# Two graph layers on one core: the degree products spread over ten edge steps, the sums added nine steps late, the attention finished one chunk at a time

## The chip, the cores and the metric

The kernel runs on one core of one Trainium2 chip. Its time is the device time of one execution in microseconds. The kernel before takes 1850.17 us, the median of three runs from 1849.44 to 1851.53 us.

## The reference

Two graph layers run on 50,000 nodes of 256 float32 features with 12,500 edges. The first layer is an attention over the edges, the second a weighted graph convolution with self-loops and a small perceptron. Cut to what is computed:

```python
x_norm = layernorm(h) * g + b             # h = relu(layernorm(x))
q, k, v = x_norm @ Wq.T + bq, x_norm @ Wk.T + bk, x_norm @ Wv.T + bv
dk, dv = silu(edge_attr @ Wdk.T + bdk), silu(edge_attr @ Wdv.T + bdv)
attn = silu(sum(q[dst] * k[src] * dk, axis=1)) * cosine_cutoff(edge_weight)
msg = v[src] * dv * attn[:, None]
x1 = x + h + segment_sum(msg, dst) @ Wo.T + bo
# second layer, h = relu(layernorm(x1)), edges (src -> dst) plus a self-loop per node
deg = segment_sum(edge_weight, src) + 1
norm = rsqrt(deg[src]) * edge_weight * rsqrt(deg[dst])
h7 = segment_sum((h @ W)[dst] * norm, src) + h @ W / deg + b
out = x1 + relu(h7 @ W1 + b1) @ W2 + b2
```

## The kernel before

Edges are cut into 98 chunks of 128, the partitions of the chip's local memory; two chunks are a pair, so there are 49 pairs. The program has four stretches: an opening, the edge stage of the first layer (`messages`, one pair per step), the edge stage of the second layer (`messages2`, four chunks per step) and the node stage (`nodes`, 512 nodes per step). The change touches the first two.

Each engine has its own instruction list, written out by hand, and they meet only at semaphores. A Python function `messages(s)` describes one step for one engine. `Step.back(n)` is the pair that entered the pipeline n steps earlier, so step s works on several pairs at once. `run_steps` writes the first and last steps out and runs the middle ones in a hardware loop.

**The opening.** The degree of a node is a sum over edges. For every chunk VectorE makes two one-hot matrices (`hot`, L625 and L626) and TensorE multiplies them (L1178) and accumulates all 98 products in one bank. TensorE makes 48 of them, folds weights together (L1191 to L1204) and makes 50 more before its first edge step. VectorE makes 80 before its first step and 18 within steps 1 to 3. At the same time SyncE issues 98 stores of 512 KB (L394) that fill the table `sums0` with the output bias, and then one store per later use; no sum may be added before that fill has landed. Below it is called the fill.

**One edge step, for pair k.** GpSimd issues four gathers of 128 rows (L492): normalised source and destination rows come from them. VectorE takes statistics (L708, L710), ScalarE subtracts the mean (L1074, L1075), VectorE takes statistics again (L774), GpSimd raises the variance to the power of -0.5 (L523, the list calls it the power), ScalarE scales (L1054) and TensorE transposes (L1227), ScalarE copies the transposed rows to `zT` (L1024). For each chunk i of the pair TensorE then makes the edge product D (L1239), the product of keys and values (L1246, "KV" below) and the query product (L1253). ScalarE applies Silu to D (L1042, tile `ds`). VectorE multiplies keys (L718, `kd`), sums query times key (L723, `at`), ScalarE applies Silu (L1091, `sa`), and VectorE multiplies with the cutoff (L810, `aa`) and makes the message (L815, `msg`). TensorE sums messages of equal destination with equality matrices (L1269 to L1271, "S"), multiplies with Wo (L1285, "U"), ScalarE copies out (L1034, `ub`), and GpSimd adds two blocks of 128 rows to `sums0` (L488, the scatters).

TensorE's list in one step is: D, KV and query of chunk 0; transposes of chunk 1; S of the pair before; D, KV and query of chunk 1; U of two pairs before; transposes of chunk 0 of the next pair. GpSimd's list in step p is: gathers of pair p, scatters of pair p-7, power of pair p-2. The attention of both chunks is finished together at the end of VectorE's step: one Silu, one `aa`, both messages. Two buffers carry the rows of a scatter.

The loads of a pair's edge features and destinations (L370, L375) are on SyncE's list. Those of pairs 0 and 1 come first, those of pairs 2 and 3 stand between the stores of the fill, and those of pair 4 and later behind it, each with two more stores of 512 KB for the second table (L383).

```python
            for i in range(NG):
                if i in (LOADS_AT, LOADS_AT + 12):
                    load_edges(Step(2 + (i - LOADS_AT) // 12))
                sp.dma_start(group(sums0, Step(i)), rows_b).then_inc(s_fill, 16)
```

The inverse square roots of the degrees (`inverse_roots`, L681 to L687) stand behind VectorE's step 5.

## Time and profile before

| what | value |
|---|---|
| median of three runs | 1850.17 us (1849.44 to 1851.53) |
| the profiled execution | 1868.97 us |
| its span, first to last instruction | 1867.3 us |
| TensorE busy | 1629.1 us, 87% |
| VectorE busy | 1412.2 us, 76% |
| GpSimd busy | 1227.1 us, 66% |
| ScalarE busy | 1119.3 us, 59% |
| mean granted TensorE clock | 0.939 of full |

A busy share over the whole span hides that the four stretches have different limits: the profile's slices show the transfers at nine tenths or more for the first three slices of 47 us, and at seven, six and five tenths in those that follow. So the opening and the edge stage are read on their own, from windows, from the engines' timelines and from waits. In a row of a timeline stand start, length, engine, line, operation, output and input, the number of merged instructions, and in brackets the engine's idle time before it with what ended it. A float32 matmul appears as two records of TensorE. The end of a matmul is modelled.

### The profile page before, as it was taken

To read this page: it belongs to the slowest core of one execution; us is meant where nothing else is said; L and a number is where in the kernel's file an instruction comes from. 1 tells how busy PE (TensorE), PEld (TensorE's weight loads), DVE (VectorE), ACT (ScalarE), POOL (GpSimd) and SP (SyncE) were. 2 spreads that over 40 slices of the span, in tenths; PEclk is the share of its full clock that TensorE was granted. 3 is DMA by queue.
4 is the path that set the end of the run, shared out by engine and by line. 5 is a ranking of instruction groups with operands and counts; after the bars stand their busy time and mean duration, and the time that the engine had idled before them with its cause. 6 is when DMAs were issued, how large, how long until landed. Compare 5 with 4: busy or idle time off the path is not lost.

```text
span 1867.3 us, 29386 instructions
## 1 busy us (share of the span) xinstructions
PE 1629.1 (87%) x6406; PEld 1099.9 (59%) x6406; DVE 1412.2 (76%) x5503; ACT 1119.3 (60%) x2092; POOL 1227.1 (66%) x864
## 2 busy tenths in 40 slices
PE   8788999999999967676675169999999999999998
PEld 4355666666666635454454046666666666666666
DVE  7986777777777639777776497888888888888873
ACT  0155555556666522222222378889889889989984
POOL 3246777777777646888887765666666666666650
PEclk9999999999999987878777679999999999999999
DMA  9997666666666655555556678999999999999981
GB/s 370 419 415 244 175 175 174 174 174 175 177 177 185 195 136 115 118 111 108 113 115 126 136 200 248 255 266 271 269 268 268 267 270 267 267 268 269 274 230 75
DMA packets 148023, 398.67 MB, mean 214 GB/s; under 512 B 20144, under 2 KB 56756, under 8 KB 147974
## 3 DMA queue, kind: packets, MB, share of 16 engines
q1 hardware_dynamic: 89830, 280.18, 43.8%
q0 software_dynamic: 56416, 115.46, 32.8%
q10 hardware_dynamic: 1728, 2.50, 0.4%
q8 instruction: 15, 0.25, 0.1%
q14 instruction: 34, 0.28, 0.0%
HBM read 217.84 MB, written 180.23 MB: 213 GB/s over the span
## 4 chain that ended last, share of the span: by engine, by line
PE 27%; POOL 25%; issue 13%; DMA 11%; DVE 10%; ACT 7%; another core or an unknown queue 4%; SPq 3%; ACTq 0%; DVEq 0%; POOLq 0%
POOL sums_dram L488 9%; DMA out_dram<-cg 8%; PE bank L1361 6%; PE bank L1350 6%; POOL kept L578 6%; PE bank L1246 4%; POOL cg L492 4%; POOL b_rs L484 4%; ACT z L1054 4%; DVE cg L958 3%; PE bank L1178 2%; PE bank L1253 2%; PE bank L1340 2%; SPq L394 1%
## 5 line engine op out<-in xcount | busy, mean ns | idle before, releaser
L1350 PE MATMUL bank<-kept,w 128*128 128x512 f32 x784 | 355.4, 596 | 0.0
L1361 PE MATMUL bank<-w_sb,kept 128*128 128x256 f32 x1568 | 354.3, 379 | 0.0
L578 POOL TENSOR_TENSOR kept<-kept 128x1024 f32<-128x1024 f32 x98 | 232.4, 2371 | 183.4 <-DVE cg L958 183.4
L1361 PEld LDWEIGHTS bank<-w_sb,kept 128*128 128x128 f32 x1568 | 297.9, 190 | 81.9 <-issue 46.4
L488 POOL DMA_INDIRECT sums_dram<-ub,sidx x148 | 244.1, 1649 | 91.3 <-issue 42.3
L1314 PE MATMUL bank<-cg,en 128*128 128x256 f32 x386 | 132.8, 489 | 124.7 <-issue 80.6
L484 POOL TENSOR_TENSOR b_rs<-b_ve,minus_half 128x8 f32<-128x8 f32 x102 | 210.5, 2064 | 28.7 <-DVE b_ve L975 28.7
L1350 PEld LDWEIGHTS bank<-kept,w 128*128 128x128 f32 x784 | 142.6, 192 | 142.3 <-issue 142.3
L1145 ACT ACTIVATE kept<-kept,b_nb,b_rs 128x256 f32<-128x256 f32 x392 | 202.2, 588 | 21.9 <-DVE b_nb L948 21.9
L1246 PE MATMUL bank<-qkv_w,zT 128*128 128x512 f32 x392 | 192.0, 612 | 21.4 <-DVE msg L815 18.0
L1135 ACT ACTIVATE kept<-kept,b_nb,b_rs 128x256 f32<-128x256 f32 x392 | 202.2, 589 | 12.5 <-DVE b_nb L948 12.5
L1314 PEld LDWEIGHTS bank<-cg,en 128*128 128x128 f32 x386 | 94.2, 251 | 157.6 <-issue 139.6
L986 DVE SCALAR_TENSOR_TENSOR kept<-cg,dinv,kept 128x256 f32<-128x256 f32 x392 | 164.0, 480 | 5.1 <-issue 2.2
L1126 ACT ACTIVATE kept<-bank 128x1024 f32<-128x1024 f32 x98 | 100.4, 1024 | 90.6 <-PE bank L1340 90.6
L492 POOL DMA_INDIRECT cg<-in_x_dram,node_i x98 | 105.4, 1075 | 74.3 <-ACT cg L1075 48.7
L1340 PE MATMUL bank<-identity,kept 128*128 128x128 f32 x784 | 105.3, 278 | 54.7 <-DVE kept L986 54.4
L958 DVE TENSOR_TENSOR cg<-kept,bank 128x1024 f32<-128x1024 f32 x98 | 119.6, 1220 | 41.1 <-PE bank L1361 34.7
L1246 PEld LDWEIGHTS bank<-qkv_w,zT 128*128 128x128 f32 x392 | 71.3, 192 | 132.2 <-issue 72.3
L1024 ACT ACTIVATE zT<-bank 128x512 f32<-128x512 f32 x98 | 58.3, 595 | 144.2 <-PE bank L1227 79.6
L718 DVE TENSOR_TENSOR kd<-bank,ds 128x256 f32<-128x256 f32 x98 | 41.6, 424 | 130.4 <-PE bank L1246 73.2
L963 DVE BATCH_NORM_STATS2 b_st<-kept 128x6 f32<-128x256 f32 x392 | 137.0, 412 | 0.0
L967 DVE BATCH_NORM_STATS2 b_st<-kept 128x6 f32<-128x256 f32 x392 | 136.1, 410 | 0.0
(172 smaller groups left out, 3260.3 us busy)
## 6 DMA issues: line engine op xcount, KB each, us to landing
sums_dram<-cg SPq DMA_DIRECT2D x196, 512.0 KB
kept<-in_x_dram SPq DMA_DIRECT2D x97, 512.0 KB, 5.7
kept<-sums_dram POOLq DMA_DIRECT2D x97, 512.0 KB, 9.8
cg<-sums_dram SPq DMA_DIRECT2D x97, 512.0 KB, 8.7
out_dram<-cg SPq DMA_DIRECT2D x97, 512.0 KB, 9.8
row_d<-in_dst_dram SPq DMA_DIRECT2D x49, 128.0 KB
row_k<-keys_dram SPq DMA_DIRECT2D x24, 256.0 KB
row_s<-in_src_dram SPq DMA_DIRECT2D x24, 256.0 KB
```

The lines of the kernel that those rows point to most:

```text
L484: pool.tensor_tensor(to, var, minus_half[:, 0:width].rearrange("p (a b) -> p a b", b=1), ALU.pow).then_inc(done, 1)
L488: pool.indirect_dma_start(sums, bass.IndirectOffsetOnAxis(idx, 0), rows, None, bounds_check=bound, compute_op=ALU.add).then_inc(done, 16)
L492: pool.indirect_dma_start(to, None, table, bass.IndirectOffsetOnAxis(idx, 0), bounds_check=bound, oob_is_err=True).then_inc(done, 16)
L578: pool.tensor_tensor(X1[k.slot(8)], X[k.slot(4)], H[k.slot(2)], ALU.add).then_inc(g_xh, 1)
L958: dve.tensor_tensor(OUT[k.slot(2)], X1[k.slot(8)], bank[:, to:to + 2, :].rearrange("p a b -> p (a b)"), ALU.add).then_inc(g_fin, 1)
L986: ins = dve.scalar_tensor_tensor(AG[k.slot(2)][:, at0], S1[k.slot(4)][:, at0], dinv[:, bass.ds(k.value(0, G) + j, 1)], H1[k.slot(2)][:, at ...
L1135: ins = act.activation(H1[k.slot(2)][:, j * D:(j + 1) * D], X1[k.slot(8)][:, j * D:(j + 1) * D], ACT.Relu, bias=b_nb[k.back(-4).slot(2)][: ...
L1145: ins = act.activation(H[k.slot(2)][:, j * D:(j + 1) * D], X[k.slot(4)][:, j * D:(j + 1) * D], ACT.Relu, bias=b_nb[k.slot(2)][:, j, :], sc ...
L1246: ins = pe.matmul(bank[:, 2 + i, :], zT[i][:, c, :], qkv_w[:, c, D:3 * D], start=(c == 0), stop=(c == KC - 1))
L1314: ins = pe.matmul(bank[:, 6 * q + to // 2, (to % 2) * D:(to % 2 + 1) * D], EN[q][i][:, to * P:(to + 1) * P], H1e[q][:, i, :], start=(i == to),
L1350: ins = pe.matmul(bank[:, 2 + m, :], w01[:, c, m * P:(m + 1) * P], hT[k.slot(2)][:, c * GN:(c + 1) * GN], start=(c == 0), stop=(c == KC - 1))
L1361: ins = pe.matmul(to, rT[k.slot(2)][:, c * GN + j * P:c * GN + (j + 1) * P], w2_sb[:, c, :], start=False, stop=(c == KC - 1), skip_group_c ...
```

## The change

Five things change.

- `hots(step)` gives VectorE and TensorE the products of a step: 10, 8, 8, 8, 11, 11, 11, 11, 10, 10. TensorE makes 18 before its first step and folds the weights. The other 80 stand within steps 2 to 9, on TensorE behind the query product of chunk 1. The one-hot matrices have six buffers instead of four, and their sum is in bank 7. `degrees()` stands behind step 10 and `inverse_roots()` behind step 12.
- GpSimd scatters pair p-9 in step p. In steps before 11 the power comes ahead of the scatters. The rows of the first eight pairs lie in eight buffers, those of later pairs in four, made from tiles that are used later.
- The attention is finished per chunk: the query products of both chunks share bank 4, ScalarE applies Silu per chunk, VectorE makes the message of chunk 0 in the middle of its step and that of chunk 1 in the next step, behind the first statistics.
- TensorE transposes chunk 0 of the next pair ahead of U.
- ScalarE issues the loads of pairs 2 to 9, three steps behind their number. SyncE's fill has no loads in it, and the first 12 stores of the second table follow it without a load between them.

```diff
-HOT_FIRST, HOT_LOOPS = 48, 80
-HOT_STEP = 6
-LOADS_AT = 72
+HOT_STEPS = (10, 8, 8, 8, 11, 11, 11, 11, 10, 10)
+HOT_RING = 6
+SCATTER_LAG = 9
+POWER_FIRST = 11
+LOADED = 10
...
+        early_ub = [UB4[:, 2 * i:2 * i + 2, :].rearrange("p a d -> p (a d)") for i in range(2)] + [
+            e[3][:, :] for e in EN] + [t[:, :] for t in row_k] + [t[:, :].bitcast(F32) for t in row_s]
+        def ub_slot(k):
+            return early_ub[k.off if k.reg is None and k.off < 8 else k.slot(4)]
...
+        def load_pair(eng, k):
+            q = k.slot(2)
+            if k.within(EP):
+                if k.past(2):
+                    pass_on(eng, (m_D, k.value(-1, 2)))
+                eng.dma_start(aT[q][0:R, :], edge_attr[:, bass.ds(k.value(0, 2 * P), 2 * P)]).then_inc(m_attr[q], 16)
+                if k.past(2):
+                    pass_on(eng, (m_eq, k.value(-1)))
+                eng.dma_start(row_d[q][:, :],
+                              dst[bass.ds(k.value(0, 2 * P), 2 * P)].rearrange("(a e) -> a e", a=1)
+                              .broadcast_to([P, 2 * P])).then_inc(m_row[q], 16)
...
+        def hots(step):
+            return range(sum(HOT_STEPS[:step]), sum(HOT_STEPS[:step + 1]))
...
+                if s.past(LOADED):
+                    load_pair(sp, s)
...
-            run_steps(sp, EP, LATER, 2, 2, load_edges, start=LATER)
+            run_steps(sp, EP, LATER, 2, LOADED - LATER, load_edges, start=LATER)
...
-                k = p - 7
+                if p < POWER_FIRST:
+                    power(p - 2)
+                k = p - SCATTER_LAG
...
-                        scatter_add(sums0, sidx[:, 2 * k + i:2 * k + i + 1], UB[2 * (k % 2) + i], last_row, m_sc)
-                k = p - 2
+                        scatter_add(sums0, sidx[:, 2 * k + i:2 * k + i + 1], ub_slot(Step(k))[:, i * D:(i + 1) * D],
+                                    last_row, m_sc)
+                if p >= POWER_FIRST:
+                    power(p - 2)
...
             def hot(k):
-                q = k.slot(4)
-                if k.past(4):
-                    dve.wait_ge(s_hotmm, k.value(-3))
-                dve.tensor_scalar(hot_p[q][:, :], iota_p[:, :], col(pkey, k), col(ew_f, k), ALU.is_equal, ALU.mult)
-                dve.tensor_scalar(hot_c[q][:, :], iota_c[:, :], col(ckey, k, 1), None, ALU.is_equal).then_inc(s_hot, 1)
+                q = k % HOT_RING
+                if k >= HOT_RING:
+                    dve.wait_ge(s_hotmm, k - HOT_RING + 1)
+                dve.tensor_scalar(hot_p[q][:, :], iota_p[:, :], pkey[:, k:k + 1], ew_f[:, k:k + 1], ALU.is_equal, ALU.mult)
+                dve.tensor_scalar(hot_c[q][:, :], iota_c[:, :], ckey[:, k:k + 1, 1], None, ALU.is_equal).then_inc(s_hot, 1)
...
+                own = hots(s.off) if s.reg is None and s.off > 0 else ()
...
-                    dve.tensor_tensor_reduce(junk[i][:, :], bank[:, 4 + 3 * i, 0:D], KD[i][:, :], 1.0, 0.0,
+                    dve.tensor_tensor_reduce(junk[i][:, :], bank[:, 4, i * D:(i + 1) * D], KD[i][:, :], 1.0, 0.0,
...
+                def message(k, i):
+                    q = k.slot(2)
+                    dve.wait_ge(m_sa, k.value(0, 2) + i + 1)
+                    dve.tensor_tensor(aa[q][:, i:i + 1], sa[q][:, i:i + 1], cut[:, bass.ds(k.value(0, 2) + i, 1)],
+                                      ALU.mult).then_inc(m_aa, 1)
+                    dve.wait_ge(m_aa, k.value(0, 2) + i + 1)
+                    if k.past(1):
+                        dve.wait_ge(m_S, k.value(0))
+                    dve.scalar_tensor_tensor(MSG[i][:, :], bank[:, 2 + i, D:2 * D], aa[q][:, i:i + 1],
+                                             DS[i][:, D:2 * D], ALU.mult, ALU.mult).then_inc(m_msg, 1)
+                if f.within(EP):
+                    message(f, 1)
...
                     ins.then_inc(m_eq, 1)
+                    message(m, 0)
...
+                for j in own[:HOT_RING]:
+                    hot(j)
...
-                    dve.wait_ge(m_sa, m.value(1))
-                    dve.tensor_tensor(aa[q][:, :], sa[q][:, :], pair_of(cut, m), ALU.mult).then_inc(m_aa, 1)
-                    dve.wait_ge(m_aa, m.value(1))
-                    if m.past(1):
-                        dve.wait_ge(m_S, m.value(0))
-                    for i in range(2):
-                        dve.scalar_tensor_tensor(MSG[i][:, :], bank[:, 2 + i, D:2 * D], aa[q][:, i:i + 1],
-                                                 DS[i][:, D:2 * D], ALU.mult, ALU.mult).then_inc(m_msg, 1)
...
+                if s.reg is None and s.off == 2:
+                    for j in range(4):
+                        subtract_first(j // 2, j % 2)
+                if s.reg is None and s.off == 3:
+                    for j in range(2):
+                        bias_row(j)
+                    folded()
+                for j in own[HOT_RING:]:
+                    hot(j)
...
-                    degrees()
...
-                if s.reg is None and s.off == 5:
+                if s.reg is None and s.off == len(HOT_STEPS):
+                    degrees()
+                if s.reg is None and s.off == len(HOT_STEPS) + 2:
                     inverse_roots()
...
+                def attended(k, i):
+                    act.wait_ge(m_at, k.value(0, 2) + i + 1)
+                    if k.past(2):
+                        act.wait_ge(m_aa, k.value(-2, 2) + i + 1)
+                    act.activation(sa[k.slot(2)][:, i:i + 1], at[k.slot(2)][:, i:i + 1], ACT.Silu).then_inc(m_sa, 1)
...
+                if s.back(5).within(EP):
+                    attended(s.back(5), 1)
...
-                    if k.past(2):
-                        act.wait_ge(m_sc, k.value(-1, 32))
-                    act.activation(UB4[:, 2 * k.slot(2):2 * k.slot(2) + 2, :].rearrange("p a d -> p (a d)"),
-                                   bank[:, 6, :], ACT.Copy).then_inc(m_UB, 1)
+                    if k.past(8):
+                        act.wait_ge(m_sc, k.value(-3, 32))
+                    act.activation(ub_slot(k), bank[:, 6, :], ACT.Copy).then_inc(m_UB, 1)
...
+                if s.reg is None and 2 <= s.off - 3 < LOADED:
+                    load_pair(act, s.back(3))
...
                     turned(1)
+                    attended(s.back(4), 0)
...
-            run_steps(act, EP, MESSAGE_STEPS, 2, 2, messages)
...
+            run_steps(act, EP, MESSAGE_STEPS, 4, 9, messages)
...
+            for step in range(2):
+                for k in hots(step):
+                    hot(k)
...
-            with pe.Fori(HOT_FIRST // 4, HOT_LOOPS // 4) as reg:
-                for u in range(4):
-                    hot(Step(u, reg, 4))
-            for k in range(HOT_LOOPS, EC):
-                hot(Step(k))
...
-                    if k.past(1):
-                        pe.wait_ge(m_at, k.value(-1, 2) + i + 1)
+                    if i or k.past(1):
+                        pe.wait_ge(m_at, k.value(0, 2) + i)
                     for c in range(KC):
-                        ins = pe.matmul(bank[:, 4 + 3 * i, 0:D], zT[i][:, KC + c, :], qkv_w[:, c, 0:D],
+                        ins = pe.matmul(bank[:, 4, i * D:(i + 1) * D], zT[i][:, KC + c, :], qkv_w[:, c, 0:D],
                                         start=(c == 0), stop=(c == KC - 1))
...
+                if s.reg is None and s.off >= 2:
+                    for k in hots(s.off):
+                        hot(k)
+                if t.within(EP):
+                    turn(t, 0)
                 if u.within(EP):
                     pe.wait_ge(m_ST, u.value(1))
                     if u.past(1):
                         pe.wait_ge(m_UB, u.value(0))
-                    else:
-                        pe.wait_ge(s_deg, 1)
                     for i in range(2):
                         for c in range(KC):
                             ins = pe.matmul(bank[:, 6, i * D:(i + 1) * D], ST[u.slot(2)][:, i, c, :], wo_t[:, c, :],
                                             start=(c == 0), stop=(c == KC - 1))
                     ins.then_inc(m_U, 1)
-                if t.within(EP):
-                    turn(t, 0)
-            run_steps(pe, EP, MESSAGE_STEPS, 2, 2, messages)
+            run_steps(pe, EP, MESSAGE_STEPS, 2, 6, messages)
             def messages2(s):
                 k, a = s, s.back(1)
```

The built programs differ as follows. GpSimd, around the first scatter, before (`cg` and `kept` are the gathered rows, `rs` is the power, `sums_dram` the table):

```order
L492 DMA cg<-in_x_dram,node_i 128x256
L492 DMA kept<-in_x_dram,node_i 128x256
L492 DMA cg<-in_x_dram,node_i 128x256
L492 DMA kept<-in_x_dram,node_i 128x256
L488 DMA sums_dram<-ub,sidx 50304x256 x2
L523 TENSOR_TENSOR rs<-ve,minus_half 128x6
L492 DMA cg<-in_x_dram,node_i 128x256
```

and now:

```order
L507 DMA cg<-in_x_dram,node_i 128x256
L507 DMA kept<-in_x_dram,node_i 128x256
L507 DMA cg<-in_x_dram,node_i 128x256
L507 DMA kept<-in_x_dram,node_i 128x256
L545 TENSOR_TENSOR rs<-ve,minus_half 128x6
L503 DMA sums_dram<-ub,sidx 50304x256 x2
L507 DMA cg<-in_x_dram,node_i 128x256
```

The first scatters stand two gather groups later, and the power has moved ahead of them.

TensorE in a step of the edge stage without degree products, before (`wd_t,aT` is D, `qkv_w,zT` are KV and query, `wo_t,stt` is U, `identity,z_0` the transposes of chunk 0):

```order
L1239 MATMUL bank<-wd_t,aT 128x512
L1246 MATMUL bank<-qkv_w,zT 128x512 x2
L1253 MATMUL bank<-qkv_w,zT 128x256 x2
L1285 MATMUL bank<-wo_t,stt 128x256 x4
L1227 MATMUL bank<-identity,z_0 128x128 x4
L1239 MATMUL bank<-wd_t,aT 128x512
```

and in step 9, with its products, now:

```order
L1256 MATMUL bank<-wd_t,aT 128x512
L1263 MATMUL bank<-qkv_w,zT 128x512 x2
L1270 MATMUL bank<-qkv_w,zT 128x256 x2
L1202 MATMUL bank<-kept 128x392 x10
L1244 MATMUL bank<-identity,z_0 128x128 x4
L1305 MATMUL bank<-wo_t,stt 128x256 x4
L1256 MATMUL bank<-wd_t,aT 128x512
```

Ten products stand between the query product and the transposes, and U is behind these.

VectorE around the end of a step, before (`fst` to `sidx` are the scatter's row numbers, `st` the statistics, `kd` the keys of the next pair's chunk 0):

```order
L807 TENSOR_TENSOR sidx<-fst,dump_f 128x2
L810 TENSOR_TENSOR aa<-sa,cut 128x2
L815 SCALAR_TENSOR_TENSOR msg<-bank,aa,ds 128x256 x2
L708 BN_STATS st_0<-cg 128x6 x2
L710 BN_STATS st_0<-kept 128x6 x2
L718 TENSOR_TENSOR kd<-bank,ds 128x256
```

and now, behind step 12:

```order
L699 RECIPROCAL kept<-kept 128x392
L700 TENSOR_TENSOR kept<-kept 128x392
L701 TENSOR_TENSOR kept<-kept 128x392
L702 TENSOR_SCALAR kept<-kept 128x392
L703 TENSOR_TENSOR kept<-kept 128x392
L704 TENSOR_TENSOR dinv<-kept 128x392
L705 TENSOR_TENSOR dinv<-dinv 128x392
L724 BN_STATS st_0<-cg 128x6 x2
L726 BN_STATS st_0<-kept 128x6 x2
L745 TENSOR_TENSOR aa<-sa,cut 128x1
L750 SCALAR_TENSOR_TENSOR msg<-bank,aa,ds 128x256
L734 TENSOR_TENSOR kd<-bank,ds 128x256
```

One `aa` of two columns and two messages became an `aa` of one column and one message on this side of the statistics' row; the other message stands in the middle of the step. The seven instructions on 392 columns are the inverse square roots.

## Rows read from the trace of the kernel before

**Rows 1.** Windows of the whole span: length, busy time by engine, granted clock, DMA share, GB/s.

```profile
60.00:156.00 96.00, 71.09 (x237) 39.98 (x236) 79.39 (x308) 38.62 (x79) 34.48 (x31) 0.91 1.03 413
204.00:481.00 277.00, 265.45 (x1152) 176.33 (x1152) 197.55 (x937) 165.56 (x360) 212.34 (x169) 1.00 0.63 175
```

**Rows 2.** Groups of lines, 20 to 60 us: busy us, mean ns, idle before.

```profile
L626 DVE TENSOR_SCALAR kept<-iota_c,ckey 128x392 f32<-128x392 f16 x51 | 21.3, 418 | 0.0
L625 DVE TENSOR_SCALAR kept<-kept,ew_f 128x128 f32<-128x128 f16 x51 | 17.8, 350 | 6.9 <-PE bank L1178 6.8
```

**Rows 3.** Timeline, 59 to 104 us: start, length, instruction, idle before it.

```profile
59.64 10.04 PE L1178 MATMUL bank<-kept 128*128 128x392 f32 x30
...
100.49 0.57 DVE L674 TENSOR_SCALAR kept<-bank 128x392 f32<-128x392 f32 x1 [1.55 <-PE bank L1178]
...
103.25 0.75 DVE L708 BATCH_NORM_STATS2 st<-cg 128x6 f32<-128x256 f32 x2
```

**Rows 4.** Timeline around the end of the fill.

```profile
140.46 1.03 POOL L492 DMA_INDIRECT kept<-in_x_dram,node_i  x1 [0.30 <-issue]
...
147.63 0.75 DVE L708 BATCH_NORM_STATS2 st<-cg 128x6 f32<-128x256 f32 x2 [0.20 <-DMA kept<-in_x_dram,node_i]
...
153.63 1.64 POOL L488 DMA_INDIRECT sums_dram<-ub,sidx  x1 [12.15 <-DMA sums_dram<-cg]
...
159.65 0.42 DVE L718 TENSOR_TENSOR kd<-bank,ds 128x256 f32<-128x256 f32 x1 [10.61 <-PE bank L1246]
```

**Rows 5.** Timeline of GpSimd after the fill.

```profile
158.70 1.13 POOL L492 DMA_INDIRECT cg<-in_x_dram,node_i  x1 [0.19 <-issue]
...
164.16 1.81 POOL L488 DMA_INDIRECT sums_dram<-ub,sidx  x1 [0.30 <-issue]
...
169.42 1.13 POOL L492 DMA_INDIRECT cg<-in_x_dram,node_i  x1 [0.19 <-issue]
```

**Rows 6.** TensorE groups up to 203.8 us, and the next instruction of this line.

```profile
L1246 PE MATMUL bank<-qkv_w,zT 128*128 128x512 f32 x64 | 34.2, 660 | 5.5 <-DVE msg L815 4.3 <-ACT zT L1024 1.2
```

**Rows 7.** Timeline of TensorE from 203.8 us.

```profile
203.86 1.98 PE L1246 MATMUL bank<-qkv_w,zT 128*128 128x512 f32 x4 [1.00 <-DVE msg L815]
```

**Rows 8.** Timeline of one edge step in the loop, 400 to 413 us.

```profile
400.91 1.96 PE L1246 MATMUL bank<-qkv_w,zT 128*128 128x512 f32 x4 [0.61 <-DVE msg L815]
...
405.34 1.02 PE L1239 MATMUL bank<-wd_t,aT 65*128 65x512 f32 x2
...
408.57 0.60 ACT L1042 ACTIVATE ds<-bank 128x512 f32<-128x512 f32 x1 [1.81 <-remote]
...
410.12 0.42 DVE L718 TENSOR_TENSOR kd<-bank,ds 128x256 f32<-128x256 f32 x1 [2.66 <-remote]
...
410.51 0.60 PE L1227 MATMUL bank<-identity,z 128*128 128x128 f32 x4
...
411.67 0.60 ACT L1024 ACTIVATE zT<-bank 128x512 f32<-128x512 f32 x1 [0.28 <-issue]
...
411.72 0.88 DVE L815 SCALAR_TENSOR_TENSOR msg<-bank,aa,ds 128x256 f32<-128x256 f32 x2
...
412.40 1.98 PE L1246 MATMUL bank<-qkv_w,zT 128*128 128x512 f32 x4 [0.43 <-ACT zT L1024]
```

**Rows 9.** Waits of 204 to 481 us: engine and line, what for, us, times, longest.

```profile
ACT ds L1042 <- remote: 43.2, 24, 2.3
...
POOL rs L523 <- DVE ve L802: 23.1, 24, 1.5
```

**Rows 10.** Timeline of TensorE in the last edge steps.

```profile
638.94 1.97 PE L1246 MATMUL bank<-qkv_w,zT 128*128 128x512 f32 x4
...
660.78 1.97 PE L1246 MATMUL bank<-qkv_w,zT 128*128 128x512 f32 x4
```

**Rows 11.** Timeline of VectorE, inverse square roots of the degrees.

```profile
121.98 2.59 DVE L681 RECIPROCAL kept<-kept 128x392 f32<-128x392 f32 x1
...
127.96 0.74 DVE L708 BATCH_NORM_STATS2 st<-cg 128x6 f32<-128x256 f32 x2
```

71 lines of the change are left out of this document (15 added, 56 removed).

## The prediction

> **What bounds the kernel now.** I read four views in this order. The table of windows shows that the first 156 us run the transfers at their limit, 413 GB/s with the DMA engines at 1.03 of the window, while TensorE idles a quarter of the time, and that the loop of the edge stage has TensorE at 265 of 277 us [rows 1]. The timeline of the opening shows what the early idle time is. VectorE and TensorE do nothing but degree products up to 67 us, and then the pipeline runs into the fill: the first scatter waits 12.15 us for a store and goes at 153.63, and VectorE stands 10.61 us before the keys at 159.65 [rows 4]. The timeline of one loop step shows the second limit. TensorE is late for KV by 0.4 to 0.6 us, once for the message and once for `zT`, and both arrive together, at 412.2 to 412.3 [rows 8]. Last, the waits: ScalarE stands 43.2 us in 24 steps before `ds` of chunk 1, and GpSimd 23.1 us before the power, so it is nearly full too [rows 9].
>
> One number ties these together. 64 records of KV stand before 203.86 us, four to a chunk, so at that time pair 8 starts its KV, in step 12 [rows 6, 7]. Pair 48 starts at 660.78 us [rows 10]. These 40 steps took 456.9 us, 11.42 each. What follows (second stage, nodes) has the same instructions and starts when the last scatter has landed, so I price it at nothing. It would cost if the new buffers held back a first load of the second stage; `row_k` and `row_s` are free at the scatters of pairs 4 to 7, some 500 us before.
>
> **The opening.** VectorE's part first. A pair of one-hot matrices costs 0.65 us: 40 us less 6.9 idle, by 51 [rows 2]. Before, step 4 starts at 103.25 with 98 of them made [rows 3]. Now 34 are made by then. 64 fewer are 41.6 us, the wait of 6.8 us behind TensorE's folding goes [rows 2], and so do the 1.55 us before the degrees and about 1.5 us of `degrees()` itself, at 0.57 or less for each of three instructions [rows 3]. Step 4 starts at 51.8 us.
>
> From there TensorE paces. A step of it without a wait is 10.92 us, half of 638.94 to 660.78 [rows 10]. A product is 0.67 us: 30 records, 15 products, in 10.04 us [rows 3]. S and U have 768 and 1024 columns; at KV's rate, 1024 columns in 1.8 us, they are 1.35 and 1.8 us. Step 4 has neither and eleven products: 15.2 us. Step 5 has no U: 17.0. Steps 6 and 7 are 18.3 each, 8 and 9 with ten products 17.6 each. Step 10 then starts at 155.8 and ends at 166.7.
>
> Meanwhile the fill. By its end GpSimd has gathered for two more pairs, 1.05 MB, and two more pairs of loads have gone, 0.4 MB. At 413 GB/s [rows 1] that is 3.5 us, so the fill ends at 157.1. The loads now leave from ScalarE. I add their bytes all the same, since the DMA share is 1.03 whoever issues [rows 1]. The Trainium skill ("DMA: Bandwidth & Descriptors", section "Issuing engines are not separate DMA queues") says the same: transfers from any engine run on the same 16 DMA engines and interleave. By a queue with bandwidth of its own the sum would be 1 us better; no row here tells the two apart better than that share.
>
> GpSimd comes to pair 0's scatters in step 9 and is held until 157.1, with gathers up to pair 9 and the power of pair 7 behind it. Two scatters are 3.7 us (153.63 to 158.70 [rows 4, 5] less a power of 1.4), four gathers 5.46 us (158.70 to 164.16 [rows 5]). The last gather of pair 10 starts at 164.9, and one that started at 140.46 held VectorE until 147.63 [rows 4], so it lands at 172.1. VectorE's step 11 starts there, and chunk 1's message is out 2.0 us later, at 174.1. TensorE would want it for S at 170.7 (166.7, D 0.9, KV, query and transposes 3.1): a wait of 3.4 us. Pair 8's KV is at 166.7 + 3.4 + 10.92 + 0.9 = 181.9 us, 22.0 us earlier than 203.86.
>
> One thing leaves its cover. The inverse roots take VectorE 5.98 us, 121.98 to 127.96 [rows 11]. Before, they lie ahead of the fill's end, which hides them. Now they stand behind step 12, on an engine that everything queues behind: the next statistics, the message of chunk 1, the keys. VectorE idles 79 of 277 us [rows 1], 3.3 us a step, less 0.3 for the second `aa` and its semaphore. With a faster step it is 2 to 2.6. I take 4 us as lost. It could be 0 if gathers are late anyway, or 6. The opening is worth 18 us, within 8 and 26.
>
> **The steady step.** KV of chunk 0 no longer waits for a message made at the end of the same chain: that message now stands in the middle of VectorE's step, 6 us ahead. `zT` needs the transposes, now ahead of U, which gives 1.8 us, and it needs ScalarE. There the chain stays: `ds` of chunk 1 starts 7.66 us behind KV, from it to `zT` are 3.10 us less the Silu of 0.2 and an idle 0.28, `zT` is 0.60, and KV starts 0.14 behind: 11.0 us [rows 8]. The late start of `ds` is odd. D began at 405.34 and lasts about 1 us; `ds` came at 408.57, and the keys at 410.12 although their KV should have been out [rows 8]. The trace doesn't say what holds TensorE's signals there. The other floors are TensorE's 10.92 and GpSimd's 10.72 (158.70 to 169.42 [rows 5]). So the period lies between 10.92 and the old 11.42, and a new wait could take it beyond. I take 11.1, nearest to ScalarE's chain. Forty steps by 0.32 are 13 us.
>
> The second half of the attention adds a wait on VectorE: the message of chunk 1 waits for ScalarE's Silu, which stands behind `zT`. Queued behind it are the keys of the next chunk 0, and TensorE's S waits too. I count the Silu out at 11.2 us behind KV and VectorE there at 11.9, so it costs nothing. The shared bank makes a query product wait for the other chunk's sum; that is done 2 to 7 us before. ScalarE's 16 load issues fall in steps of 11 to 18 us in which it has 7 us of work.
>
> **Sum.** 18 + 13 = 31 us. The profiled execution goes from 1868.97 to 1838, and with its 19 us over the median the runs go from 1850.17 to 1819 us.
>
> **The rivals.**
> 1. Clean: late signals vanish with the stalls, the period is 10.92 (20 us), and GpSimd catches up with the roots hidden (24): 44 us, 1806. For it: 638.94 to 660.78 ran so [rows 10]. Against: there GpSimd gathered nothing.
> 2. The period stays at 11.42, since the late `ds` sets it and not the message: 18 us, 1832. For it: both inputs of KV at 412.40 were late by the same amount [rows 8].
> 3. The opening gives nothing: extra transfers and the queue on GpSimd hold pair 8 where it was, and only the steady step gains 13: 1837.
> 4. Slower. VectorE, in order, stands at the top of every step for the Silu of chunk 1. ScalarE gives it only after `zT`, and if the sum of chunk 1 is late by the same signals (keys at 9.2 us behind KV [rows 8]), the loop sum, Silu, message, S, D, `ds`, keys, sum closes in one step. The price is what the loop exceeds 11.42 by; at 0.45 us a step it has eaten the opening's 18 us. At 1 us it is 40 - 18 = 22 us slower: 1872.
> 5. It doesn't do what it says: bank 7, the six buffers or the order hold the products back, so that they still precede the steps; then 5 us are left: 1845.
>
> **How the numbers follow.** The forecast has 0.50, with 1808 to 1830 as its own range. Rival 1 has 0.20, rival 2 0.16, rival 3 0.05, rival 4 0.05, rival 5 0.04. The time is 1819 us. The range 1797 to 1841 holds the forecast and rivals 1 to 3 with most of their spread. A change is told from none at 0.2% of the time, 3.7 us. Faster is all but rival 4 and a third of rival 5: 0.93; the same 0.02; slower 0.05.
>
> **What would show it.** VectorE's step 4 near 52 us, and TensorE's steps 6 and 7 at 18 us with hardly a wait. First scatter near 157 us. Pair 8's KV at 180 to 186 us: this tells rival 3. A stall of 3 to 4 us on TensorE's S behind that, at the step in which the inverse roots run. KV to KV at 11.1 us over pairs 8 to 48, with its wait on `zT` and none on the message; `ds` still waiting 1 to 2 us would keep my chain, none at all is rival 1. VectorE idle before `aa` of one column at the top of each step is rival 4. The forecast is wrong if the period is under 10.9 or over 11.4, or if the first scatter comes after 165 us.

## The result and the profile after

The changed kernel takes 1833.72 us, the median of four runs (1831.30 to 1834.30). The kernel before takes 1850.59 us (1849.44 to 1851.53, four runs). The ratio is 0.991, with a 95% interval of 0.9894 to 0.9926. The forecast was 1819 us in a range of 1797 to 1841. The sign and the range hold, but 16.9 us came where 31 were forecast.

The profiled execution after took 1834.30 us and lies within its runs. The one of before took 1868.97 us and does not lie within 1849 to 1852. So I profiled the kernel before once more (1851.07 us) and the changed kernel twice more. The second and third of these ran on a chip on which the kernel before takes 1871.7 and 1872.7 us, and there the changed kernel takes 1856.7 (ratio 0.9921, interval 0.9904 to 0.9938) and 1858.7 us (0.9925, 0.9906 to 0.9944). The change is therefore worth about the same at two levels. The first trace of before, by its time, belongs to the upper one. In this table each column compares two traces whose kernel before runs at the same level. All numbers are in us, rounded one by one, and a gain is positive.

| stretch | before, own trace to changed, second trace | before again to changed, first trace |
|---|---|---|
| start to KV of pair 8 | 203.9 to 181.6: +22.2 | 201.8 to 183.0: +18.8 |
| KV of pair 8 to KV of pair 48 | 456.9 to 460.3: -3.4 | 439.8 to 437.6: +2.2 |
| last KV to the first gather of the second stage | 29.8 to 42.2: -12.4 | 29.4 to 41.6: -12.2 |
| from there to the first node step | 355.8 to 355.5: +0.3 | 356.2 to 354.9: +1.3 |
| node stage | 820.9 to 814.4: +6.5 | 822.3 to 815.6: +6.7 |
| span | 1867.3 to 1853.9: +13.4 | 1849.4 to 1832.7: +16.7 |
| period, pairs 12 to 44 | 11.47 to 11.41 | 11.00 to 10.83 |

The windows of the changed kernel, first trace, with the columns of [rows 1]:

```profile
52.00:161.00 109.00, 104.85 (x390) 63.79 (x389) 88.86 (x375) 42.34 (x95) 33.93 (x30) 1.00 1.03 416
209.00:469.00 260.00, 260.00 (x1153) 178.56 (x1152) 204.12 (x961) 170.05 (x385) 215.22 (x169) 1.00 0.67 187
621.00:662.00 41.00, 20.10 (x86) 13.40 (x84) 9.34 (x36) 6.03 (x11) 18.32 (x12) 0.83 0.49 76
```

TensorE is busy for 96% of the opening under a fill that still runs at the limit, where it was 74% [rows 1]. In the loop of this trace it is busy all the time. Behind the last KV it is half idle. The DMA share of the opening is 1.03 as before, now with 16 of the loads issued by ScalarE. [rows 1] alone could not show that the issuer makes no difference; these two rows together agree with it, for these loads.

The opening, from the timeline of VectorE, GpSimd and TensorE (start, length, engine, line, what, and the idle time before):

```profile
52.59 0.75 DVE L724 BATCH_NORM_STATS2 st<-cg 128x6 f32<-128x256 f32 x2
...
154.64 1.76 POOL L545 TENSOR_TENSOR rs<-ve,minus_half 128x6 f32<-128x6 f32 x1 [11.56 <-DVE ve L834]
158.02 1.67 POOL L503 DMA_INDIRECT sums_dram<-ub,sidx  x1 [1.62 <-DMA sums_dram<-cg]
...
165.95 1.01 POOL L507 DMA_INDIRECT kept<-in_x_dram,node_i  x1 [0.30 <-issue]
...
183.01 1.88 PE L1263 MATMUL bank<-qkv_w,zT 128*128 128x512 f32 x4
```

The first row answers to 103.25 in [rows 3]. The first scatter's wait for the fill is 1.62 us where it was 12.15 [rows 4], and the last row is pair 8's KV, 203.86 in [rows 7].

The step of the loop, ScalarE in the first trace, then in the second, for the same two instructions:

```profile
401.75 0.60 ACT L1046 ACTIVATE zT<-bank 128x512 f32<-128x512 f32 x1
404.26 0.60 ACT L1071 ACTIVATE ds<-bank 128x512 f32<-128x512 f32 x1 [0.17 <-PE bank L1256]
407.28 0.60 ACT L1046 ACTIVATE zT<-bank 128x512 f32<-128x512 f32 x1 [2.42 <-PE bank L1244]
409.83 0.58 ACT L1071 ACTIVATE ds<-bank 128x512 f32<-128x512 f32 x1
```

```profile
403.14 0.60 ACT L1046 ACTIVATE zT<-bank 128x512 f32<-128x512 f32 x1 [0.40 <-remote]
404.20 0.60 ACT L1071 ACTIVATE ds<-bank 128x512 f32<-128x512 f32 x1
407.11 0.60 ACT L1046 ACTIVATE zT<-bank 128x512 f32<-128x512 f32 x1 [2.31 <-PE bank L1244]
411.18 0.60 ACT L1071 ACTIVATE ds<-bank 128x512 f32<-128x512 f32 x1 [1.43 <-remote]
```

And TensorE of the second trace around the first of these:

```profile
398.05 1.88 PE L1263 MATMUL bank<-qkv_w,zT 128*128 128x512 f32 x4
399.76 1.03 PE L1270 MATMUL bank<-qkv_w,zT 128*128 128x256 f32 x4
400.63 0.60 PE L1244 MATMUL bank<-identity,z 128*128 128x128 f32 x4
401.06 1.89 PE L1305 MATMUL bank<-wo_t,stt 128*128 128x256 f32 x8
402.79 1.02 PE L1256 MATMUL bank<-wd_t,aT 65*128 65x512 f32 x2
403.79 1.98 PE L1263 MATMUL bank<-qkv_w,zT 128*128 128x512 f32 x4
405.61 1.03 PE L1270 MATMUL bank<-qkv_w,zT 128*128 128x256 f32 x4
```

The transposes end at 401.23. ScalarE is free for `zT` at 402.74, but their signal is recorded at 403.12. `zT` starts at 403.14, and KV follows it at 403.79. In all 32 steps from pair 12 to pair 44 of this trace `zT` of chunk 0 starts within 0.11 us behind that signal. It is a late signal as in [rows 8], but of the transposes; the part on the steady step comes back to it. It is the signal that is late and not the work: U and D stand behind the transposes and last 2.6 us, but `ds` of that D starts 1.06 us behind `zT`. In the first trace the signal is recorded at 401.65, 0.29 us behind the start of the last transpose's record, and the same copy starts at 401.75.

What TensorE waited for from 233 to 590 us, in the view of waits (us in total, times, longest). First before, then the changed kernel, second trace:

```profile
PE bank L1246 <- DVE msg L815: 11.3, 19, 0.9
PE bank L1246 <- ACT zT L1024: 2.1, 4, 0.7
```

```profile
PE bank L1263 <- ACT zT L1046: 9.5, 18, 1.0
```

The wait for the message is gone and a wait for `zT` of nearly the same size stands in its place. In the trace of before taken again this view has one wait of 0.2 us in the same window, and in the changed kernel's first trace none.

Behind the last KV, GpSimd of the kernel before, taken again, and then of the changed kernel, first trace:

```profile
652.25 1.55 POOL L488 DMA_INDIRECT sums_dram<-ub,sidx  x1 [6.15 <-ACT ub L1034]
...
658.70 1.55 POOL L488 DMA_INDIRECT sums_dram<-ub,sidx  x1 [3.04 <-ACT ub L1034]
...
665.08 1.55 POOL L488 DMA_INDIRECT sums_dram<-ub,sidx  x1 [2.99 <-DMA sums_dram<-ub,sidx]
...
670.94 1.10 POOL L492 DMA_INDIRECT cg<-sums_dram,node_i  x1 [2.46 <-DMA sums_dram<-ub,sidx]
```

```profile
630.43 1.69 POOL L503 DMA_INDIRECT sums_dram<-ub,sidx  x1 [6.40 <-DMA sums_dram<-en,sidx]
...
637.03 1.55 POOL L503 DMA_INDIRECT sums_dram<-ub,sidx  x1 [3.06 <-ACT ub L1064]
...
643.42 1.55 POOL L503 DMA_INDIRECT sums_dram<-en,sidx  x1 [2.99 <-DMA sums_dram<-ub,sidx]
...
656.32 1.55 POOL L503 DMA_INDIRECT sums_dram<-ub,sidx  x1 [3.01 <-DMA sums_dram<-en,sidx]
...
662.15 1.10 POOL L507 DMA_INDIRECT cg<-sums_dram,node_i  x1 [2.44 <-DMA sums_dram<-ub,sidx]
```

Each pair's scatters wait until those of the pair before have landed, 6.4 us apart when nothing else runs. The last copy (`ub`) of the changed kernel is out at 636.9, and four pairs are scattered behind that time, where it was two. The last scatter starts 35.7 us behind the last KV instead of 23.5.

The node stage, the wait of VectorE at its first loop step, in the trace of before taken again (from 1110 to 1160 us):

```profile
DVE b_rs L945 <- issue: 6.2, 1, 6.2
```

The changed kernel has no such row. One node step takes 13.0 us before (12.4 in the first trace) and 7.9 after, and the eight steps around it take 68.8 us (67.3) and 62.1.

### The profile page after: what moved, and what is told of

The parts are those of the page before. It is cut to its first block, busy times and chain, and to the rows that moved or that the text cites. A ratio compares the mean times of both kernels' runs of the same rounds, so it can differ in the third digit from the quotient of the medians.

```text
span 1832.7 us, 29028 instructions
## 1 busy us (share of the span) xinstructions
PE 1613.2 (88%) x6406; PEld 1102.1 (60%) x6406; DVE 1419.0 (77%) x5552; ACT 1128.3 (62%) x2142; POOL 1229.1 (67%) x864
## 4 chain that ended last, share of the span: by engine, by line
PE 35%; POOL 27%; DMA 17%; DVE 11%; issue 7%; SPq 1%; POOLq 0%; ACT 0%; DVEq 0%; ACTq 0%
DMA out_dram<-cg 13%; POOL sums_dram L503 9%; PE bank L1263 8%; POOL kept L600 8%; POOL b_rs L499 5%; PE bank L1256 4%; PE bank L1305 4%; PE bank L1270 4%; POOL cg L507 4%; DVE cg L980 4%; PE bank L1379 3%; PE bank L1368 3%; DMA sums_dram<-ub,sidx 2%; PE bank L1244 2%; PE bank L1202 2%
## 5 line engine op out<-in xcount | busy, mean ns | idle before, releaser
L503 POOL DMA_INDIRECT sums_dram<-ub,sidx x96 | 163.0, 1698 | 54.7 <-issue 27.0
L1263 PE MATMUL bank<-qkv_w,zT 128*128 128x512 f32 x392 | 185.4, 594 | 0.1
L602 POOL DMA_DIRECT2D kept<-sums_dram x98 | 89.8, 916 | 65.9 <-POOL kept L600 61.7
L545 POOL TENSOR_TENSOR rs<-ve,minus_half 128x6 f32<-128x6 f32 x49 | 69.3, 1414 | 95.1 <-DVE ve L834 86.3
```

The costliest lines, as they stand in the source:

```text
L503: pool.indirect_dma_start(sums, bass.IndirectOffsetOnAxis(idx, 0), rows, None, bounds_check=bound, compute_op=ALU.add).then_inc(done, 16)
L1263: ins = pe.matmul(bank[:, 2 + i, :], zT[i][:, c, :], qkv_w[:, c, D:3 * D], start=(c == 0), stop=(c == KC - 1))
```

## The experiments

The first four ran together on a chip where the kernel before takes 1850.54 us (19 runs, 1847.89 to 1853.68).

**The kernel before, again.** No edit.

> The kernel before, once more, for a second trace. The first profiled execution took 1868.97 us and the three timed ones 1850.17; the trace of the changed kernel (1834.30) stands 34.7 us below that trace, the runs 16.9. Theory A (the 19 us are in the edge stage: the late TensorE signals are a matter of the one execution): if this one takes 1850, its period over pairs 8 to 48 is 10.95 us and not 11.42, and everything else is as before. Theory B (the period of 11.42 belongs to the kernel): KV to KV is 11.4 us again, and an execution of 1850 us has its 19 us less elsewhere, in the second stage and the nodes.

It took 1851.07 us, with a period of 11.00 us. In this trace too the signals of S arrive late, 1.6 to 3.1 us behind the start of its last matmul where 0.29 is prompt, but TensorE waits only 0.2 us for it between 233 and 590 us. So theory A is right on where the time went: the first trace's 19 us lie in the edge stage, 17.1 us between pairs 8 and 48 and 2.1 ahead of them.

**The steady part alone.** The kernel before, with

```diff
+                if s.back(5).within(EP):
+                    attended(s.back(5), 1)
...
                     turned(1)
+                    attended(s.back(4), 0)
...
+                if t.within(EP):
+                    turn(t, 0)
                 if u.within(EP):
...
-                if t.within(EP):
-                    turn(t, 0)
```

and VectorE's `message` as in the change.

> The kernel before with only the attention per chunk and the transposes ahead of U; the products, the lag of seven and the loads stay. Theory A (before's runs have a period of 10.95 us, so the steady step had next to nothing to give): 1845 to 1850 us, 0 to 5 less than before, with a period of 10.83. Theory B (the period was 11.42 in the runs too): 40 steps by 0.59 us are 24 us, so 1827 us. In both, no message stands before KV and TensorE never waits in the loop.

It took 1852.90 us (10 runs), a ratio of 1.0016 (1.0006 to 1.0025): a trifle slower than before. The period is 11.05 us and not 10.83, and TensorE still waits for `zT`, 2.5 us in 7 times between 233 and 590 us. By itself this half gives nothing. Both theories missed the period and the time.

**The opening alone.** The changed kernel, with the three edits above taken back.

> The changed kernel with the attention of both chunks finished together again and U ahead of the transposes; the spread products, the lag of nine and the loads stay. Theory A (all of the 17 us come from the opening less the tail): 1834 to 1840 us. Theory B (the steady step carries 24 us of the difference and the opening, less 12 us of tail, hardly anything): 1850 to 1858 us. KV of pair 8 near 185 us and the last scatter 35 us behind the last KV in both.

It took 1847.64 us (10 runs, 1840.73 to 1850.96), ratio 0.9979 (0.9967 to 0.9992). KV of pair 8 came at 185.9 us, the period is 11.04, and the last scatter started 35.2 us behind the last KV. The time lies between the two theories. From its trace beside that of before taken again: 15.9 us won in the opening, 3.7 lost from pair 8 to 48, 11.6 lost in the tail, 4.4 won in the node stage. These and 0.4 in the second stage are the 5.5 us by which this execution is shorter; the medians differ by 2.9. The tail eats most of the opening. The two halves give 0.5 us when added and 14 to 17 together; why is not settled (below).

**The inverse roots spread.**

```diff
-                if s.reg is None and s.off == len(HOT_STEPS) + 2:
-                    inverse_roots()
+                if s.reg is None and 0 <= s.off - len(HOT_STEPS) - 2 < len(ROOTS):
+                    inverse_root(s.off - len(HOT_STEPS) - 2)
...
-            run_steps(dve, EP, MESSAGE_STEPS, 2, 6, messages)
+            run_steps(dve, EP, MESSAGE_STEPS, 2, 16, messages)
```

> The changed kernel with the seven instructions of the inverse roots one to a step, at the end of VectorE's steps 12 to 18. In the changed kernel the step from pair 9's KV to pair 10's is 15.4 us instead of 10.83. If the roots alone did that, this step is 10.9 us, the time is 4.5 us less (1829), and all later starts are 4.5 us earlier. Rival: the step is long because gathers still arrive late after the fill, and the roots only fill a wait; then it stays at 13 to 15 us and the time within 1 us of the changed kernel.

It took 1843.27 us (4 runs), ratio 0.9955 (0.9939 to 0.9972). The long step is gone, 11.6 instead of 15.35 us, so the rival with late gathers falls. The forecast of 1829 us missed: the period is 11.06, and the time cannot be set against 1833.7. The price of the roots was settled by the last pair of kernels below.

The next four ran together where the kernel before takes 1851.46 us (25 runs).

**A longer written-out list alone.** Only the line `run_steps(dve, ..., 2, 16, messages)` of the edit above.

> The changed kernel with VectorE's first steps written out up to step 23 instead of 13, as the kernel with the spread roots had them, and with the roots left in one piece behind step 12. That kernel had TensorE's signals 2 to 3 us late and a period of 11.06 us, the changed kernel has them on time and 10.83. Theory P (the long step at the roots lets GpSimd and the stores fall into a phase in which nothing is late): on time, 10.83, 1833 us. Theory L (the way the list is written out or placed decides): late, 11.05, 1840 to 1844 us.

It took 1845.97 us (10 runs, 1842.32 to 1850.25), ratio 0.9974 (0.9962 to 0.9987). The step at the roots is 15.75 us. The next fifteen steps take 10.83 to 10.93 us although S's signals come 1.1 to 2.6 us behind its last matmul; then they come at up to 3.0 and steps vary from 10.9 to 11.5. Neither theory holds as it was put: the signals were late already when the step was 10.83.

**The roots in one piece, behind step 20.**

> The same, with the roots in one piece behind step 20. Theory P: signals late and steps of 11.05 from step 13 to 20, one step of about 15 us at step 20, and behind it signals on time and steps of 10.83: 1835 us. Theory L: no difference between the steps ahead of 20 and those behind it, 11.05 in both if the list decides for late, 10.83 in both if not.

It took 1847.52 us (10 runs), ratio 0.9981 (0.9967 to 0.9994), where theory P had 1835. The long step moved with the roots: 17.9 us in place of about 11. Ahead of it the last five steps were 10.9 to 11.4, behind it three were 10.83 and the next six below 11.0. A pause of VectorE gives the other engines a lead and so some short steps, as theory P has it, but it does not pay for itself. One signal of S came at 0.4 us behind the pause, the next at 1.6 and more.

**The second table's stores at three a step.**

```diff
-                    for i in range(2):
-                        sp.dma_start(sums1[bass.ds(k.value(0, 2 * GN) + i * GN, GN), :]
+                elif s.reg is not None or s.off < LOADED + 28:
+                    zeros(s, s.value(-6, 3 * GN), 3)
```

> The changed kernel with three stores of the second table in each of steps 10 to 37 instead of two in steps 10 to 52, so that none is left for the last steps. In the changed kernel a pair's scatters start 9 to 11 us behind the ones before while stores run, and 6.45 us when alone; the last scatter starts 35.7 us behind the last KV, 12 us more than before the change. Theory T (the tail is the chain of scatters, each waiting for the landing of the one before, slowed by the stores): pairs 40 to 48 go at 6.5 to 7 us each up to the copy of pair 48 at 636, the last scatter starts near 640, the second stage begins 16 us earlier, and the time is 1818 us. Rival: three stores a step make the landing exceed 10.83 us, GpSimd waits in the loop, and the steps lose what the tail gains (28 steps by 0.5 us are 14): 1832 us. The steps without stores tell besides whether late signals need the stores.

It took 1839.26 us (4 runs, 1833.43 to 1840.49), ratio 0.9943 (0.9925 to 0.9961), which is 6.7 us less than the kernel with the longer list beside it. Both forecasts, 1818 and 1832 us, missed. Its trace is of the fastest of the four executions. In it the last scatter started 28.8 us behind the last KV, 7 us earlier than without the edit. The period is 11.01 us, so three stores a step cost nothing there, and the late signals go on in the steps that have no stores, so it is not the stores that make them late. That the tail did not shrink by 16 us has its reason on GpSimd's timeline of this kernel:

```profile
606.07 1.59 POOL L517 DMA_INDIRECT sums_dram<-ub,sidx  x1 [0.20 <-issue]
607.97 1.56 POOL L517 DMA_INDIRECT sums_dram<-ub,sidx  x1 [0.30 <-issue]
615.05 1.35 POOL L559 TENSOR_TENSOR rs<-ve,minus_half 128x6 f32<-128x6 f32 x1 [5.52 <-DVE sidx L853]
616.61 1.59 POOL L517 DMA_INDIRECT sums_dram<-en,sidx  x1 [0.20 <-issue]
```

Pair 42's scatters stand behind the power of pair 48, for which it waits 5.52 us, since VectorE gives the input only at its own step's pace. Up to there the scatters can't run ahead of the steps.

**U ahead of the transposes again.**

```diff
-                if t.within(EP):
-                    turn(t, 0)
                 if u.within(EP):
...
+                if t.within(EP):
+                    turn(t, 0)
```

> The changed kernel with U ahead of the transposes of the next chunk 0 again, and nothing else undone. If the transposes decide, `zT` comes too late for KV by 0.1 to 0.5 us in each step: period 11.0 to 11.3, time 1841 to 1850 us. Rival: the attention per chunk alone is enough: 10.83 and 1834 us.

It took 1849.51 us (10 runs), ratio 0.9990 (0.9978 to 1.0002), 3.5 us more than the kernel with the longer list beside it. Period (11.09 us) and time lie in the ranges of the first case, but not for its reason alone: TensorE waits for `zT` only 1.3 us in 4 times between 233 and 590 us. The shortest steps are 10.92 us, as in the kernel before, and not 10.83. With the transposes first, a step without waits is 0.09 us shorter, about 4 us over 45 steps. TensorE spends the difference in KV of chunk 0: the query product follows 1.81 us behind it in the traces of before, and 1.72 in the changed kernel's first.

The last ones ran where the kernel before takes 1871.7 us (11 runs, 1867.80 to 1875.69).

**The changed kernel again.**

> The changed kernel once more, beside the variants. Its first trace has no TensorE signal late in the loop and steps of 10.83 us; all seven other traces have signals 2 to 3 us late from 180 us on and steps of 11.0 to 11.1, the kernel with only a longer written-out VectorE list too. Theory C (the code of the changed kernel has something that the variants lose): on time again, 10.83 and 1831 to 1835 us. Theory D (the late signals belong to the execution or the chip and not to the kernel): 11.0 to 11.1 us, a time of 1839 to 1846, and then the variants are to be compared with this time and not with 1833.7.

It took 1856.70 us (6 runs), with a period of 11.41 us and signals of S at 1.5 to 3.0 us. Theory C is refuted: the code is the same as in the first trace. Theory D's mechanism holds, its time does not, since this chip is slower for both kernels. The variants of the first two groups can be compared with each other and with the kernel before only.

**Two pairs of scatters in steps 20 and 26.**

```diff
+                lag = SCATTER_LAG - sum(p > t for t in CATCH_UP)
+                if p in CATCH_UP:
+                    scatters(p - lag)
...
+                if p in CATCH_UP:
+                    scatters(p - lag + 1)
```

> The changed kernel with two pairs of scatters instead of one in GpSimd's steps 20 and 26, one pair ahead of the gathers and one behind the power, so that the lag is eight behind step 20 and seven behind step 26. Theory T (the last scatter of the changed kernel is 12 us later than before because two more pairs are left behind the last copy, at 6.45 us each): the last scatter starts 23 us behind the last KV instead of 35.7 and the time is 12 us less than that of the changed kernel run beside it. Rival: 3.7 us more in two steps of GpSimd, with 1.9 us of slack each, and a wait of up to 3 us for the landing hold VectorE and TensorE for 2 to 5 us each time: 2 to 8 us less. A third: the tail is bound by TensorE's last U and the copy and not by the chain of scatters; then nothing is gained.

It took 1856.89 us (5 runs), the same as the changed kernel beside it. The last scatter starts 23.5 us behind the last KV instead of 36.3: the 12 us of the tail are the lag of nine, as theory T says. But the last KV comes 12.7 us later. Steps of 14.2 and 13.7 us stand at the first double step and 16.5 and 12.4 at the second, and TensorE waits for the message there:

```profile
298.51 0.46 PE L1296 MATMUL bank<-eq,msg 128*128 128x128 f32 x2 [3.11 <-DVE msg L760]
```

The rival is right, and with 11 us for both together it costs more than the 2 to 5 us each that I gave it. The gain of the tail was paid in the loop.

**The same with the roots spread.**

> Both: the two double steps of scatters and the inverse roots one instruction to a step (steps 12 to 18). If the roots cost the changed kernel 4.5 us and nothing else takes their place, 4 to 5 us less than the kernel with the double steps alone. If the long step at the roots is what gives some dozen steps of 10.83 us behind it (as in the kernels with the longer list, where steps 10 to 18 ran at 10.83 and later ones at 11.05), half of that is given back: 1 to 3 us less.

It took 1853.04 us (5 runs), ratio 0.9901 (0.9887 to 0.9915), 3.9 us less than the one before it and the lowest time on this chip, 3.7 us less than the changed kernel. From pair 8 to pair 12 it needs 46.2 us instead of 51.5. The roots in one piece cost about 4 us.

**The changed kernel a third time.**

> The changed kernel a third time. Its second trace had TensorE's signals late and a period of 11.41 us, at 1856.7 us, where the kernel before takes 1871.7. So the late signals belong to the execution, and chips differ by some 20 us in what they cost. Open is what the variants that ran where the kernel before takes 1850 to 1851 us are to be compared with. If this run falls on such a chip with late signals: period 10.98 to 11.06, 1840 to 1846 us (ratio 0.995 to 0.997), and then the kernel with the longer list and the changed one are the same. If signals are on time: 10.83 and 1831 to 1836 us (ratio 0.991). If it is late and nevertheless at 0.991 to 0.992, the longer written-out list of VectorE costs 10 us by itself. On a chip like that of the second trace: 1853 to 1860 us and a ratio of 0.992.

It took 1858.72 us (6 runs) on the same chip, period 11.37 us. The last of the expected cases came true. What the changed kernel takes with late signals on a chip of the 1850 level was not measured.

## Why the prediction was right in sign and half in size

**The opening.** This part held nearly number by number. VectorE's step 4 started at 52.59 us (51.8 forecast), the first scatter at 158.02 (157.1), the last gather of pair 10 at 165.95 (164.9), pair 8's KV at 183.0, 181.6 and 183.2 us in three traces (181.9). Two errors cancelled: TensorE's steps 4 to 9 took 17.2, 17.2, 19.0, 18.9, 18.2 and 18.2 us where 15.2, 17.0, 18.3, 18.3, 17.6 and 17.6 were worked out, 4.7 more in all, and the stall of 3.4 us at S did not come (11.1 and 10.9 from pair 6 to 8), since TensorE was itself so much later. The 4.7 us are mostly a wait that I had left out. I let TensorE pace these steps, but it waited 4.2 us, in 7 times, for VectorE's one-hot matrices. Step 5 was also added up wrongly: without U it is 16.5 us by its own terms and not 17.0. That slip changed nothing, since I placed pair 8 by its gathers. At the roots' step TensorE waited for a message at S for 2.6 us, where I had looked for 3 to 4. The roots were given 4 us. Spreading them gave 3.9 in the kernel with the double steps, and their step exceeds the first trace's period by 4.5 us. So the term of 18 us was right against the trace of before (22.2 less the roots), and 3 us too large against the trace taken again (18.8 less the roots).

**The steady step.** This is the first step that failed: "The period lies between 10.92 and the old 11.42 ... I take 11.1. Forty steps by 0.32 are 13 us." The old 11.42 belonged to the one execution; the runs I subtracted from had 11.00. There 0.17 us a step were to be had, and these came in the first trace: 32 steps by 0.17 are 5.4 us, and with the roots in between pairs 8 to 48 gained 2.2. Where the old period was 11.47 the new one is 11.41, and with the roots the 40 steps lost 3.4 us. The mechanism that I named as odd and then left out of the sum decided. The message left the path, but `zT` for chunk 0 waits for the transposes' signal, which is as late as D's was, so 11.3 us of waits for the message became 9.5 us for `zT`.

That lateness is new with the change. In both traces of the kernel before, and in that of the opening alone, the signal of these transposes comes 0.29 us behind the start of the last one in each of 32 steps (pairs 12 to 44). In the changed kernel with U ahead of them again it is 0.35 in the middle. In the nine other traces with the transposes ahead of U, the first one of the changed kernel left aside, the medians are 2.0 to 2.3 us. So the order that I had credited with 1.8 us gave it back in a signal later by 1.7 to 2.0. It is rival 2 by its result, but only in part by its reason: rival 2 had the late `ds` set the period. In the step shown above `ds` of chunk 1 also waited, 1.38 us, and ScalarE was free for `zT` only 0.40 us ahead of its start; in other steps it had been free for up to 1.5 us. The price of `zT` in the forecast assumed a prompt signal. On the other side, 10.83 us lies below my floor of 10.92: I read TensorE's floor from a step with U ahead of the transposes, and the new order is 0.09 us shorter. By the forecast's own test the period was wrong at both levels, under 10.9 in the first trace and over 11.4 in the second (the third, at 11.37, just passes).

**What follows.** The second step that failed: "What follows has the same instructions and starts when the last scatter has landed, so I price it at nothing." The start itself moved. I worked out the lag of nine only where it helped, at the fill, and not at the end, where two more pairs wait behind the last copy. The unit stands in the trace: 6.43 us a pair (637.03 to 656.32 for three), 12.9 for two; 12.2 and 12.4 were measured, and the catching-up kernel took away 12.8. This is the largest miss of the sum.

**The node stage** gained 6.5 us that I had not forecast, nearly all of it in eight steps around one stall of VectorE on its own instructions when it enters the node loop. The stall stands in all three traces of a kernel with before's opening (5.6, 6.2 and 6.3 us) and in none of the eleven of a kernel with the new one, also where the attention was taken back. The node loop's own code is the same in all of them; the lists ahead of it differ. What in them decides was not tested.

**The rest** held. No message stands before KV in any trace of the changed kernel. VectorE does not wait for chunk 1's Silu at the top of the step, so rival 4 did not come. No trace shows a cost of the new query bank or of the loads on ScalarE. The loop of 10.83 us in the first trace is the first half of rival 1.

**The sum again.** By the first trace: 18.8 + 2.2 - 12.2 + 1.3 + 6.7 = 16.8 us (16.7 before rounding) against 16.9 measured. Of my 31 us, 10 were missing between start and pair 48, and 12 in the tail; the node stage and the second stage gave 8 back. So 1833.7 lies close to rival 2's 1832, but in the first trace for another reason than rival 2's. That the range held is in part luck: without the 8 us that nobody forecast the time would have been about 1842, just outside it.

**Open.** Why TensorE's signals are late is not settled. They are on time in one trace only, the changed kernel's first: S's came 0.29 us behind the start of its last matmul in every step of the loop. In the other thirteen the median is 2.2 to 2.8 us and the longest 3.7, and behind the last gathers they are on time again. In the kernels with double steps of scatters they were at 0.3 us for two steps behind each of them, so either how GpSimd's work lies against TensorE's has a part in it, or that TensorE had itself just been held up: in the long step of the roots, where TensorE also waits, S's signal came at 0.43 or 0.44 us in seven of the eight late traces that have the new opening and the roots in one piece. Nor are all signals late. In the second trace of the changed kernel D and KV of chunk 0 are at 0.60 and 0.61 us (medians, from the start of the last matmul) as in its first, while D, KV and the query of chunk 1 are at 2.4, 3.5 and 2.8, where the first has 0.61, 0.61 and 0.39. It is not the code alone (the same kernel has both), not the stores of the second table, and not the clock, which was granted in full in the loop of both. One observation goes with it: the first trace of the changed kernel holds 19,804 records of finished transfers, the others 14,910 to 15,624, and they lack records from the first 22 us on (251 to 338 against 447), long before the loop. Whether recording delays the signals, or both have one cause, was not tried. Open also is whether the two halves need one another or whether the change is worth only 5 us on a chip of the 1850 level with late signals, as the kernel with the longer list suggests.

## What to carry to other kernels

A pipeline made deeper to get past a full resource at its start pays the depth again at its end: multiply the added lag by the spacing of the last items, here 2 by 6.43 us, before counting the gain. Check that the profiled execution lies within the timed runs before taking a period from it; here the trace was 19 us above them, and nearly all of that stood in the very steps that the change was to improve. When two inputs arrive equally late, do not price the removal of one before the reason for the other's lateness is known. And an instruction moved forward in a list helps its reader only if its signal comes earlier too: here 1.8 us of place in the list met 1.7 to 2.0 us of later signal in nine traces of ten.

## What the runs showed of the hardware

- Chips differ for the same kernel: 1850.5 and 1851.5 us on two, 1871.7 and 1872.7 on a third, in 10 to 25 runs each. Between two traces of before that are as far apart, 17.1 of 17.9 us lie between the KVs of pairs 8 and 48; the node stage differs by 1.4.
- TensorE's completion can reach ScalarE and VectorE up to 3.7 us late (S in the first trace of before) while the work behind it goes on. VectorE stood 44.7 us in 22 steps before `msg` for S's signal, longest 2.4, from 250 to 500 us of the changed kernel's second trace. Which signals are late depends on the order of TensorE's list: that of the same transposes came at 0.29 us with U ahead of them and at 2.0 to 2.3 with U behind.
- A KV product whose input was ready held TensorE for 1.71 us (398.05 to 399.76 above), one that waited for its copy for 1.82 (403.79 to 405.61).
- One engine stalled 5.6 to 6.3 us on its own instruction list at the entry of a loop that the change did not touch, and did not when its list ahead of it was another.
